# Mamba state groups of a fused kernel: the group spread by matmul becomes a fourth scaled group

## The reference, cut to what matters

```python
xi, z = split(x @ in_w.T)                       # 256 channels each
xc = silu(causal_conv4(xi) + cb)
dt, Bm, Cm = split(xc @ xp_w.T, [8, 8 + 16])    # 16 states
delta = softplus(dt @ dtw + dtb)
A = -exp(A_log)
# per token: state h[256 channels, 16 states]
h = exp(delta * A) * h + (delta * u) * B         # u is xc
y = sum_over_states(h * C)
y = (y + u * D) * silu(z)
x = y @ ow.T
```

## Time and profile before

| | us |
|---|---|
| median of 3 runs without a profile | 1412.18 (1408.93 to 1414.27) |
| span of the profiled execution | 1427.8 |
| its busy time: PE / DVE / ACT / POOL | 1234.0 / 1133.5 / 1042.2 / 960.0 |
| first scan to end of last scan | 636.6 to 1413.1 |

### The profile page before, as it was taken

One profiled execution on the slowest core, in us unless ns is written; L12 is line 12 of the kernel. 1 busy time (PEld: TensorE's weight loads), 2 busy tenths in 40 slices (PEclk: granted clock), 3 DMA queues, 4 the chain that ended last, 5 costly groups with the idle time before them and its releaser, 6 DMA issues. The chain is left out here.

```text
span 1427.8 us, 21449 instructions
## 1 busy us (share of the span) xinstructions
PE 1234.0 (86%) x6427; PEld 612.9 (43%) x6427; DVE 1133.5 (79%) x1639; ACT 1042.2 (73%) x1809; POOL 960.0 (67%) x916
## 2 busy tenths in 40 slices
PE   6377599999628999898999999999999999999876
PEld 3361144444415566634444444444444444444332
DVE  6857599999676222248999999999999999999996
ACT  3337599999452223269889999998999899989871
POOL 7651411111463623238999999999999999999985
PEclk9786799999859999999999999999999999999987
DMA  2022223333218103244143414341444243414410
GB/s 65 20 92 77 81 81 114 109 121 98 60 35 301 48 19 121 74 116 106 47 105 90 114 50 95 89 118 55 97 93 101 61 108 89 96 50 105 92 52 15
DMA packets 89708, 123.56 MB, mean 87 GB/s; under 512 B 17141, under 2 KB 48576, under 8 KB 89224
## 3 DMA queue, kind: packets, MB, share of 16 engines
q1 hardware_dynamic: 83048, 103.92, 27.3%
q0 software_dynamic: 6560, 18.44, 4.3%
HBM read 96.18 MB, written 26.92 MB: 86 GB/s over the span
## 5 line engine op out<-in xcount | busy, mean ns | idle before, releaser
L2304 DVE TENSOR_TENSOR_SCAN hs<-decay,dbx 128x512 f32<-128x512 f32 x512 | 589.0, 1203 | 21.2 <-ACT decay L2187 6.8
L1871 POOL TENSOR_TENSOR hcm<-hs,Cc 128x1024 f32<-128x1024 f32 x192 | 453.2, 2371 | 20.4 <-DVE hs L2304 11.9
L2187 ACT ACTIVATE decay<-dtr,a_cur 128x512 f32<-128x512 f32 x512 | 351.9, 712 | 11.0 <-DVE hs L2304 10.7
L1992 PEld LDWEIGHTS dbx<-ident_sb,scaled 128*128 128x128 f32 x1536 | 175.9, 141 | 258.2 <-DVE hs L2304 137.4
L1992 PE MATMUL dbx<-ident_sb,scaled 128*128 128x128 f32 x1536 | 238.7, 280 | 34.7 <-DVE hs L2304 33.5
L2165 ACT ACTIVATE scaled<-duT,BT 128x256 f32<-128x256 f32 x506 | 224.9, 497 | 10.3 <-PE dbx L1992 10.3
L1864 POOL TENSOR_TENSOR hck<-hs,Cc 128x512 f32<-128x512 f32 x128 | 164.1, 1282 | 36.3 <-DVE hs L2304 36.3
L1989 PE MATMUL dbx<-du,spread_sb 128*128 128x512 f32 x256 | 140.2, 630 | 2.8 <-DVE hs L2304 2.8
L921 ACT ACTIVATE ex<-tt 128x1024 f32<-128x1024 f32 x128 | 137.2, 1072 | 6.1 <-DVE tt L971 5.0
L1919 PE MATMUL slots<-XT,w_tap 128*128 128x512 f32 (+1 forms) x240 | 123.3, 601 | 2.3 <-PEq L1311 2.3
L1854 POOL TENSOR_SCALAR scaled<-duT,BT 128x256 f32<-128x256 f32 x256 | 118.6, 489 | 0.0
(11 more groups left out here) (348 smaller groups left out, 2018.9 us busy)
## 6 DMA issues: line engine op xcount, KB each, us to landing
dtr<-dt_turn SPq DMA_DIRECT2D x60, 512.0 KB, 8.5
Cc<-bc_turn SPq DMA_DIRECT2D x256, 64.0 KB, 2.0
dt_turn<-dt SPq DMA_DIRECT2D x15, 512.0 KB, 2.8
Bb<-bc_turn SPq DMA_DIRECT2D x64, 64.0 KB, 2.0
conv_row<-in_conv_row SPq DMA_DIRECT2D x4, 512.0 KB, 5.8
shares_of_tokens<-zeros SPq DMA_DIRECT2D x2, 1024.0 KB, 9.7
w_rg<-in_w_rg SPq DMA_DIRECT2D x8, 256.0 KB
w_ru<-in_w_ru SPq DMA_DIRECT2D x8, 256.0 KB
```

Source lines behind the costliest of these rows:

```text
L1871: nc.gpsimd.tensor_tensor(hcm[:, (m - 1) % MR:m % MR + 1, :], hs[:, q % HR:p % HR + 1:p - q, :], Cc[:, k:k + 1, :].broadcast_to([P, 2, 512 ...
L1992: last = nc.tensor.transpose(dbx[bank_of[p]][:, P * kk:P * kk + P], scaled[:, (b + k) % 2, kk, g, :, :].rearrange("p j c -> p (j c)"), ide ...
L2187: nc.scalar.activation(dec[:, p % DR, :], dtr[:, b % 2, g, :], ACT.Exp, scale=a_cur[:, 4 * g + k:4 * g + k + 1]).then_inc(s_dec, 1)
L2304: nc.vector.tensor_tensor_scan(hs[:, p % HR, :], dec[:, p % DR, :], dbx[bank_of[p]][:, :], 0.0, ALU.mult, ALU.add).then_inc(s_sc, 1)
```

## The change

Group 3 is now made like the others, and units run in plain order (k = p // 8, g = p % 8). There is no spread matmul, no `times_b`, no `Bb`, no `hck`. Three `scaled` buffers go round over the groups. The sixteen small multiplications of a group are shared out anew: group 0 on VectorE, as four instructions of 128x1024 that read the transposed du straight out of PSUM (`slots[:, 1:3]`); groups 1 and 3 on ScalarE; group 2 on GpSimd. `weigh` takes all units in pairs, into a ring `hcm` of 12. `turn_du` is laid out so that each of its two PSUM banks holds two of the four token blocks for all channels. Since VectorE now reads `slots[:, 1:3]` during units 19 to 22, `xi` of h = 0 and `z` of h = 1 wait for it.

```diff
-            DR, HR, MR, KR = 8, 8, 8, 4
-            DIRECT = 3
+            DR, HR, MR, GROUPS = 8, 8, 12, 4
...
-            units = []
-            for p in range(UN):
-                units.append((DIRECT, p // 4) if p % 4 == 3 else main[len(units) - p // 4])
...
+            units = [(p // 8, p % 8) for p in range(UN)]
+            buffer_of = lambda l, n, k: (4 * (4 * l + n) + k) % 3
+            ring_of = lambda l, b, p: (UN * (4 * l + b) + p) % MR
...
@@ GpSimd
+                    own_scales = {1: (3, 4, 5), 3: (6, 7), 5: (8, 9, 10), 7: (11, 12), 9: (13, 14, 15)}
+                        for p in range(1, UN, 2):
+                            weigh(l, b, p)
...
+                            elif p in own_scales:
+                                for x in own_scales[p]:
+                                    scale_by_b(l, b, 2, x)
+                            if p == 31 and more(l, b + 1):
+                                for x in (0, 1, 2):
+                                    scale_by_b(l, b + 1, 2, x)
...
@@ TensorE: xi, z, input_of
                             elif dst is x_slot:
                                 wait(pe, s_dut, at(l, n, 1, 0))
+                                wait(pe, s_k[0], at(l, n, 16, 0))
...
                         if h == 1:
+                            pe.wait_ge(s_k[0], at(l, n, 16, 16))
...
-                        if k == DIRECT:
-                            mm(dbx[bank_of[p]][:, :], spread[:, g % 4, :], du[:, b % 2, g // 4, :], start=True, stop=True).then_inc(s_bx, 1)
-                        else:
...
+                        for kk in range(4):
+                            last = nc.tensor.transpose(dbx[bank_of[p]][:, P * kk:P * kk + P], scaled[:, buffer_of(l, b, k), kk, g, :, :].rearrange("p j c -> p (j c)"), ident[:, :])
+                        last.then_inc(s_bx, 1)
...
@@ TensorE, step: the folds
                             if not first(l, b):
-                                if v == 7:
-                                    fold_quad(l, b - 1, 2, 1)
-                                if v == 8:
-                                    fold_quad(l, b - 1, DIRECT, 1)
+                                if v == 1:
+                                    fold_quad(l, b - 1, 3, 0)
+                                if v == 6:
+                                    fold_quad(l, b - 1, 3, 1)
                                 if v in (11, 12):
                                     out_proj(l, b - 1, v - 11)
                             if v in (9, 10):
                                 start_y(l, b, v - 9)
-                            if v == 13:
+                            if v == 12:
                                 fold_quad(l, b, 0, 0)
-                            if v == 16:
+                            if v == 14:
                                 fold_quad(l, b, 0, 1)
-                            if v == 19:
-                                fold_quad(l, b, DIRECT, 0)
-                            if v == 20:
+                            if v == 18:
                                 fold_quad(l, b, 1, 0)
-                            if v == 26:
+                            if v == 22:
                                 fold_quad(l, b, 1, 1)
-                            if v == 31:
+                            if v == 25:
                                 fold_quad(l, b, 2, 0)
+                            if v == 29:
+                                fold_quad(l, b, 2, 1)
...
@@ ScalarE, step
-                                if 22 <= w < 30:
-                                    for x in (2 * (w - 22), 2 * (w - 22) + 1):
-                                        scale_by_b(l, n, 0, x)
+                                if 26 <= w < 32:
+                                    for x in (2 * (w - 26), 2 * (w - 26) + 1):
+                                        scale_by_b(l, n, 1, x)
...
+                            if w in (2, 4) and not first(l, b):
+                                for x in (w + 10, w + 11):
+                                    scale_by_b(l, b, 1, x)
...
@@ VectorE
-                    def times_b(l, b, g):
...
+                    def scale_by_b(l, n, j):
+                        if j == 0:
+                            wait(dve, s_bx, at(l, n - 1, UN, 16))
+                            dve.wait_ge(s_bt, at(l, n, 1, 1))
+                            dve.wait_ge(s_dut, at(l, n, 1, 1))
+                        TT(scaled[:, buffer_of(l, n, 0), :, :, j, :], slots[:, 1:3, :].rearrange("p i (k g c) -> p (i k) g c", k=2, c=32),
+                           BT[:, n % 2, :, j].unsqueeze(2).unsqueeze(3).broadcast_to([P, 4, 8, 32]), ALU.mult).then_inc(s_k[0], 4)
...
-                            if u % 4 == 3:
-                                times_b(l, b, u // 4)
                             scan(l, b, u)
+                            if 19 <= u < 23 and more(l, n):
+                                scale_by_b(l, n, u - 19)
```

More of the change, by code:

```diff
@@ L1718, in build_stages @@
             layer = lambda l, n: l + 1 if n >= 4 else l
-            last_of = lambda k: place[k, 7]
             more = lambda l, n: not (l == 3 and n >= 4)
-            weighed = lambda k, g: hc_after[place[k, g]]
-            hc_after = {}
-            for p, (k, g) in enumerate(units):
-                if k == DIRECT:
-                    hc_after[p] = p + 1
-                elif g % 2 == 1:
-                    hc_after[p] = hc_after[place[k, g - 1]] = p + 1
+            hc_after = [p // 2 * 2 + 2 for p in range(UN)]
             with nc.Block() as block:
@@ L1816, in _ @@
                     store_bc(0, 0)
-                    spread_direct(0, 0)
-                    for k in range(DIRECT):
+                    for k in range(GROUPS):
                         spread_c(0, 0, k)
@@ L1874, in step @@
-                    def step(l, b):
-                        for p in range(UN):
-                            if units[p][0] == DIRECT or units[p][1] % 2 == 1:
-                                weigh(l, b, p)
-                            if p < 4 and first(l, b):
-                                for x in range(4 * p, 4 * p + 4):
-                                    scale_by_b(l, b, x)
-                            if p < 2 and not first(l, b):
-                                for x in ((11, 12, 13), (14, 15))[p]:
-                                    scale_by_b(l, b, x)
-                            if p >= 28 and more(l, b + 1):
-                                for x in ((0, 1), (2, 3, 4), (5, 6, 7), (8, 9, 10))[p - 28]:
-                                    scale_by_b(l, b + 1, x)
+                        if g % 4 == 1:
+                            wait(pool, s_fm, at(l, b, 8, p // 4 - 2))
@@ L1959, in turn_du @@
                             pe.wait_ge(s_dtc, at(l, n, 1, 2))
-                        pe.wait_ge(s_dun, at(l, n, 2, h + 1))
-                        for kk in range(4):
-                            last = nc.tensor.transpose(slot[1 + h][:, P * kk:P * kk + P], du[:, n % 2, h, P * kk:P * kk + P], ident[:, :])
+                        pe.wait_ge(s_dun, at(l, n, 2, 2))
+                        for q in range(4):
+                            kk = 2 * i + q // 2
+                            last = nc.tensor.transpose(slot[1 + i][:, P * q:P * q + P], du[:, q % 2, P * kk:P * kk + P], ident[:, :])
                         last.then_inc(s_dup, 1)
@@ L2004, in fold_quad @@
                     def fold_quad(l, b, k, h):
-                        pe.wait_ge(s_hc, at(l, b, UN, weighed(k, 4 * h + 3)))
+                        p = 8 * k + 4 * h
+                        pe.wait_ge(s_hc, at(l, b, UN, p + 4))
                         for q in range(4):
-                            g = 4 * h + q
-                            src = hck[:, g % KR, :] if k == DIRECT else hcm[:, order_in_main[k, g] % MR, :]
-                            last = mm(y_bank[h][32 * q:32 * q + 32, :], fold[:, :], src, start=False, stop=((k, h) in ((DIRECT - 1, 0), (DIRECT, 1))), tile_position=(0, 32 * q), skip_group_check=True)
-                        last.then_inc(s_fk if k == DIRECT else s_fm, 1)
+                            last = mm(y_bank[h][32 * q:32 * q + 32, :], fold[:, :], hcm[:, ring_of(l, b, p + q), :], start=False, stop=(k == 3), tile_position=(0, 32 * q), skip_group_check=True)
+                        last.then_inc(s_fm, 1)
                     def step(l, b):
```

125 lines of the change are left out of this document (46 added, 79 removed).

## The result

The changed kernel takes 1454.41 us (median of 4 runs, 1452.95 to 1456.07) against 1410.56 (4 runs, 1406.99 to 1414.27): ratio 1.0316, 95% interval 1.0295 to 1.0336. The forecast was 1442, the range 1405 to 1468. It is slower by 43.9 us, 14 more than predicted.

What follows compares the result with a forecast made beforehand. VectorE and TensorE in series were taken to bound each step. Middle steps +13, clock +22 and ends -5 gave +30 us on the unprofiled median: 1442 us, range 1405 to 1468.

Steps and rivals of the forecast that it cites:

- The series of VectorE and TensorE: Middle steps: VectorE's 26.5 us, a 0.25 stall and TensorE's 22.1 in series, 48.8 against 47.8, +13 us over 13 steps.
- Its parts: VectorE from scan 7 to the fourth product 26.5 us; TensorE from the first tap to unit 7's input 21.9.
- the stall of 0.25 at unit 19: At unit 19, TensorE, with two folds and two taps since unit 14, falls behind VectorE by about 0.25 us.
- The clock: TensorE's gap before the first tap halves its clock; 1.7 us a step (0 to 3.4), +22 us over 13 steps.
- the two shorter of the three drops: Half-clock stretches of about 3.4 us in the earlier profile, the third being 6.8; taken to cost 1.7 us a step.
- rival C: At the first tap, the clock falls for 6.8 us a step: +44 us instead of +22, 1464 us; chance 12%.
- The ends: First step +3 us, step 15 -3, last step -5, after the last scan 0: together -5.
- the late group 2: First step: GpSimd has group 2 ready about 4 us after VectorE could start unit 16; net +3 us (0 to +5).
- D: TensorE does tap to unit 7 in 18 us, GpSimd sets the step at about 45.2: 1373 us; chance 17%.
- E: VectorE's new product takes 3.2 us instead of 1.2: the step +8 us, time over 1510; chance 3%.
- B: Same chain, but TensorE's clock holds with no drop: 1420 us (1407 to 1433); chance 18%.
- 4 us of waits on VectorE: From unit 26 to unit 7, VectorE's scans wait for TensorE's inputs in small pieces, about 4 us a step.

Runs made afterwards that it cites:

- the filled gap: The changed kernel with three idle 128x512 matmuls ahead of unit 24's transposes: 1422.54 us, ratio 1.0093 to the kernel before the change.
- products earlier: The changed kernel with VectorE's four products after units 17 to 20 and ScalarE's du copy two units earlier: 1405.92 us, ratio 0.9976 to the kernel before the change.
- the last experiment: The changed kernel with VectorE's products reading du's transposed copy in SBUF instead of PSUM: 1492.38 us, ratio 1.0462 to the kernel before the change.
- the gap filled with transposes: The changed kernel with unit 24's four transposes made seven times over: 1421.84 us, ratio 1.0092 to the kernel before the change.
- the kernel with the later gate: The changed kernel with early products, taps at units 23 to 26, and gate and last fold after scan 8: 1413.50 us, ratio 0.9914 to before the change.

## Why the prediction was right in its sign and 12 us short

- **The series of VectorE and TensorE.** Right. The step without the clock's fall is 48.64 in two ways of filling the gap, predicted 48.8. Over 13 steps +10.7 us (predicted +13).
- **Its parts.** VectorE from scan 7 to the fourth product 26.57 (26.5); TensorE from the tap to input 7 21.8 (21.9); the stall of 0.25 at unit 19 is not there.
- **The clock.** Mechanism right: 0.50 once a step, behind the gap at the first tap. What failed in the sum is the term "I take 1.7, by the two shorter of the three drops": it was mis-sized. The clock stays down for 6.8 us in each step, as rival C had it, and not for 3.4. Rival C's price of 3.4 a step is too high all the same, since TensorE is idle for the first part of the drop and busy for 5.5 us of it (2.08 + 3.40 in the rows above). By the filled gap it costs 2.56 a step. That is 13 x 2.56 = +33 us instead of +22, half way between the forecast and rival C.
- **The ends.** Predicted -5, measured +1.7, in this trace:

```profile
614.40 3.44 DVE L2273 TENSOR_TENSOR_SCAN hs<-decay,dbx 128x512 f32<-128x512 f32 x3 [0.88 <-PE dbx L1966]
...
646.20 3.44 DVE L2273 TENSOR_TENSOR_SCAN hs<-decay,dbx 128x512 f32<-128x512 f32 x3 [2.77 <-PE dbx L1966]
...
683.49 1.22 DVE L2273 TENSOR_TENSOR_SCAN hs<-decay,dbx 128x512 f32<-128x512 f32 x1 [0.73 <-PE dbx L1966]
...
1349.06 1.22 DVE L2273 TENSOR_TENSOR_SCAN hs<-decay,dbx 128x512 f32<-128x512 f32 x1 [0.73 <-PE dbx L1966]
...
1395.77 1.22 DVE L2273 TENSOR_TENSOR_SCAN hs<-decay,dbx 128x512 f32<-128x512 f32 x1 [1.00 <-ACT decay L2157]
```

  From the first scan to scan 7 of the second step are 69.1 us against 60.8 (636.62 to 697.43): +8.3, not +3. The 2.77 is the late group 2 that was forecast. I had left out that the first step also ends with the slow tap and its half clock, which lengthens every middle step by 3.38. The rest of the 8.3 is smaller waits for inputs, which no experiment took apart. Step 15 takes 46.7 instead of 49.4 (-2.7, predicted -3), and the last step is 4.9 shorter (predicted 5). That this one came out is in part luck: its first three `dtr<-dtr,GATE` products took 8.75 us where they took 6.66 before, which the forecast did not have, and three waits of before that went (0.66, 0.83 and 0.36 us) made up for it. Behind the last scan stands 1.0 more.
- **The sum.** 10.7 + 33.3 + 1.7 = 45.7 us, against 45.6 in the traces, 43.9 between the medians and 30 predicted. The measured time lies inside the stated range because that range reached a little beyond rival C.
- **The rivals.** D fell: TensorE's stretch is 21.8 us, not 18. At full clock, steps became shorter only by work taken out of a stretch or by an earlier start of it (products earlier, 0.86). E fell for this kernel (1199 ns), though its mechanism exists, as the last experiment shows. B did not happen by itself; it is the kernel with the filled gap, 1422.54 us, near the 1420 given. Predicted 4 us of waits on VectorE a step are 5.75 with the clock (0.90 + 2.45 + 1.04 + 0.35 + 0.28 + 0.73) and 3.3 in the gap filled with transposes (0.87 + 1.04 + 0.35 + 0.27 + 0.73).

What stays open: with the waits for the products and at the gate gone, a step still takes 46.93 us, while no engine is busy for more than VectorE's 44.41 (the row below). ScalarE's order around units 26 to 31 is one candidate, and the wait for `xc` another; no order but the two shown was tried, and what sets these 46.93 us is not shown. A step of the kernel with the later gate by windows (us, busy PE, PEld, DVE, ACT, POOL, clock, DMA):

```profile
1031.84:1078.68 46.84, 43.16 (x254) 21.05 (x253) 44.41 (x43) 43.47 (x78) 44.35 (x33) 1.00 0.36 84
```

## What to carry to other kernels

When every engine has a little slack, add up the loop in which two of them wait for each other, not their totals: a step moved ahead of a queue of inputs costs what stands behind it. If a gap ends right before that queue, put into it work that is due anyway (here one fold): here that shortened the stretch behind it and kept TensorE's clock up. An operand that could be read from PSUM or from SBUF is worth trying in PSUM where GpSimd is busy: here that was 1.20 us against 2.42 on average.

## What the runs showed of the hardware that I had not expected

- The clock fell in all middle steps at the same place: 1.34 and 2.73 us idle with one set of transposes between them (0.63), then 6.8 us at 0.50 to 0.53. Gaps of 1.34 and 1.74 us with a set of transposes and a fold between them did not bring it down, and neither did gaps of 0.77, 0.73 and 1.48 with work between them (products earlier). Float32 transposes kept it up as matmuls did.
- A VectorE product with both operands in SBUF can wait for a whole string of GpSimd operations. In the last step of the changed kernel one of 512 elements took 6.49 us beside them, and 0.69 when GpSimd was done:

```profile
1401.02 6.49 DVE L2297 TENSOR_TENSOR dtr<-dtr,GATE 128x512 f32<-128x512 f32 x1
...
1447.76 0.69 DVE L2297 TENSOR_TENSOR dtr<-dtr,GATE 128x512 f32<-128x512 f32 x1
```
